# A two-layer graph kernel: visits start at borders of pairs of steps, steps are told of in pairs, and a tile's rows are turned back ahead of the next product

## The reference

```python
def prop(h):
    return segment_sum(h[src] * norm[:, None], dst, num_segments=n)   # norm = -dinv[src] * dinv[dst]
def cheb(x, W0, W1, b):
    return x @ W0 + prop(x) @ W1 + b

h = cheb(x, W1_0, W1_1, b1)                    # 512 -> 512
h = layer_norm(h) * gamma + beta
h = where(h >= 0, h, 0.01 * h)
out = cheb(h, W2_0, W2_1, b2)
result = layer_norm(x + out)                   # no scale, no shift
```

## Time and profile before

| | us |
|---|---|
| median of 3 runs | 2662.75 |
| lowest, highest | 2658.46, 2668.54 |
| the profiled execution | 2677.57 |
| its span | 2675.8 |
| TensorE matmul busy | 2033.7 (76%) |
| GpSimd busy | 1608.5 (60%) |
| VectorE busy | 978.8 (37%) |
| ScalarE busy | 414.5 (15%) |

### The profile page before, as it was taken

The page is one execution under the profiler, slowest core; times in us unless marked ns, Lnnn a source line. Parts: engine busy times, 40 slices in busy tenths (PEclk is TensorE's granted clock), DMA queues, the critical chain, the costliest instruction groups (busy, mean ns, idle before and its releaser), DMA issues.

```text
span 2675.8 us, 28699 instructions
## 1 busy us (share of the span) xinstructions
PE 2033.7 (76%) x8006; PEld 970.8 (36%) x8006; DVE 978.8 (37%) x1503; ACT 414.5 (15%) x844; POOL 1608.5 (60%) x1721
## 2 busy tenths in 40 slices
PE   5258787877888887887884778777787878777887
PEld 5223333333333343443441333333333333333333
DVE  9943333332333333333332233333333333333333
ACT  4401111121222122121221000000000000000001
POOL 0466555666566666666654666666666666666663
PEclk7579888998899899999997889988898888989988
DMA  6576666666576677676756666766666676677674
GB/s 213 193 221 201 195 197 193 198 200 209 178 214 213 205 214 211 200 213 208 208 184 195 195 211 205 215 214 204 213 208 203 212 223 205 206 214 217 207 217 136
DMA packets 191838, 546.41 MB, mean 204 GB/s; under 512 B 32382, under 2 KB 32384, under 8 KB 191692
## 3 DMA queue, kind: packets, MB, share of 16 engines
q0 software_dynamic: 133120, 436.31, 55.3%
q10 hardware_dynamic: 44644, 81.69, 8.5%
q1 hardware_dynamic: 13928, 26.50, 2.7%
HBM read 493.03 MB, written 51.34 MB: 203 GB/s over the span
## 4 chain that ended last, share of the span: by engine, by line
PE 34%; another core or an unknown queue 30%; issue 17%; DVE 11%; ACT 5%; ACTq 1%; POOL 1%; DMA 1%; DVEq 0%; SPq 0%
PE bank L696 14%; PE bank L689 14%; PE bank L751 3%; DVE acc L1136 2%; DVE ring L890 2%; PE bank L638 2%; DVE onehot L1031 1%; DVE work L1012 1%; DVE stats L1067 1%; ACT feat L515 1%; ACT work L494 1%; ACT work L505 1%; DVE ring L892 1%; POOL ring L389 1%
## 5 line engine op out<-in xcount | busy, mean ns | idle before, releaser
L389 POOL DMA_INDIRECT ring<-table,index x1664 | 1574.8, 946 | 941.0 <-issue 468.3
L689 PE MATMUL bank<-ring,onehot 128*128 x4096 | 996.3, 399 | 166.1 <-issue 65.9
L1136 DVE TENSOR_TENSOR acc<-acc,bank 128x512 f32 x512 | 351.4, 686 | 1621.5 <-remote 829.6
L689 PEld LDWEIGHTS bank<-ring,onehot 128*128 128x128 f16 x4096 | 417.8, 102 | 697.8 <-issue 312.0
L696 PE MATMUL bank<-wA,work 128*128 128x512 f32 x784 | 414.8, 679 | 138.4 <-ACT work L494 115.7
L696 PE MATMUL bank<-wB,base_in 128*128 128x512 f32 x784 | 379.0, 628 | 38.2 <-DVE acc L1102 30.8
L1031 DVE TENSOR_TENSOR onehot<-bank,rel 128x1024 f16<-128x1024 f32 x256 | 311.6, 1218 | 0.1
L696 PEld LDWEIGHTS bank<-wA,work 128*128 128x128 f32 x784 | 166.6, 218 | 344.2 <-issue 204.8
L751 PE MATMUL bank<-diag,acc 128*128 128x128 f32 x784 | 135.4, 325 | 168.2 <-DVE acc L1136 98.7
L696 PEld LDWEIGHTS bank<-wB,base_in 128*128 128x128 f32 x784 | 154.5, 204 | 206.2 <-issue 165.5
L751 PEld LDWEIGHTS bank<-diag,acc 128*128 128x128 f32 x784 | 114.4, 224 | 192.8 <-DVE acc L1136 124.5
(11 more groups left out here) (121 smaller groups left out, 672.8 us busy)
## 6 DMA issues: line engine op xcount, KB each, us to landing
ring<-table,index POOLq DMA_INDIRECT x1664
feat<-in_x ACTq DMA_DIRECT2D x96, 256.0 KB
table<-work SPq DMA_DIRECT2D x49, 256.0 KB, 2.7
hidden_t<-feat ACTq DMA_DIRECT2D x49, 256.0 KB
table<-work ACTq DMA_DIRECT2D x49, 256.0 KB
base_in<-hidden_t ACTq DMA_DIRECT2D x49, 256.0 KB
out<-work ACTq DMA_DIRECT2D x48, 256.0 KB
acc<-in_x SPq DMA_DIRECT2D x6, 1792.0 KB, 18.6
```

The costliest lines, as they stand in the source:

```text
L389: nc.gpsimd.indirect_dma_start(out=ring[:, at * ROW:(at + 1) * ROW], out_offset=None, in_=table[l], in_offset=bass.IndirectOffsetOnAxis(ap ...
L689: last = nc.tensor.matmul(bank[n % SUM_BANKS][:, :], hot, ring[:, bass.ds(slot_at + (2 * j + half) * D, D)], start=j + half == 0, stop=j + ...
L1136: nc.vector.tensor_tensor(acc_at, acc_at, bank[n % SUM_BANKS][:, :], ALU.add).then_inc(sums_added, 1)
```

## The change

- `place(v)` is rounded down to an even number of steps, from a first place of 8.75 instead of 8. Of the 48 places 24 stay, 16 are a step later and 8 a step earlier; the distances of 5 (37 times) and 6 (10 times) become 4 (18 times) and 6 (29 times).
- `steps_done` is incremented by 2 at the last matmul of every second step instead of by 1 at every step.
- VectorE's leaky step is due at `place(v)` itself instead of one step later, and the statistics 2 steps later instead of 3.
- In `complete` of layer 0 TensorE does `turn_hidden` first and then the product.
- Four small instructions of VectorE that work out the places at run time follow suit (as many as before).

```diff
-    FIRST_PLACE = -(-STEPS // TILES) + 8 // GROUP
-    PRODUCT_LATER, LEAKY_LATER, STATS_LATER = 2, 1, 3
+    FIRST_PLACE = 35 * 64
+    PRODUCT_LATER, LEAKY_LATER, STATS_LATER = 2, 0, 2
...
-            return min(STEPS, FIRST_PLACE + (v * SPACING >> 8))
+            return min(STEPS, FIRST_PLACE + v * SPACING >> 8 & -BLOCK)
...
-                last.then_inc(steps_done[l], 1)
+                if n % BLOCK == BLOCK - 1:
+                    last.then_inc(steps_done[l], BLOCK)
...
             def complete(l, v):
-                sums_product(l, v)
                 if l == 0 and v > 0:
                     turn_hidden(v)
+                sums_product(l, v)
...
-                link(nc.vector.tensor_scalar(place_i[:, 0:1], part_i[:, :], SPACING, None, ALU.mult))
+                link(nc.vector.tensor_scalar(place_i[:, 0:1], part_i[:, :], SPACING, FIRST_PLACE, ALU.mult, ALU.add))
                 link(nc.vector.tensor_scalar(place_i[:, 1:2], place_i[:, 0:1], 8, None, ALU.arith_shift_right))
-                link(nc.vector.tensor_copy(place_f[:, 0:1], place_i[:, 1:2]))
-                link(nc.vector.tensor_scalar(place_f[:, 1:2], place_f[:, 0:1], float(FIRST_PLACE), None, ALU.add))
+                link(nc.vector.tensor_scalar(place_i[:, 0:1], place_i[:, 1:2], -BLOCK, None, ALU.bitwise_and))
+                link(nc.vector.tensor_copy(place_f[:, 1:2], place_i[:, 0:1]))
```

More of the change, by code:

```diff
@@ L100, in gnn_resnorm_kernel @@
     assert STEPS % LOADED == 0
-    assert EARLY_STEP < FIRST_PLACE and STEPS == 256 and FIRST_PLACE > 0
+    assert EARLY_STEP < FIRST_PLACE >> 8 and STEPS == 256
     assert STEPS % SUM_BANKS == 0 and BOUNDS % SLOTS == 0
@@ L904, in lateness @@
             def lateness():
-                assert all(place(v) == FIRST_PLACE + (v * SPACING >> 8) for v in range(BOUNDS)) and place(BOUNDS) == STEPS
-                link(nc.vector.tensor_scalar(place_i[:, 0:1], part_i[:, :], SPACING, None, ALU.mult))
+                assert all(place(v) == (FIRST_PLACE + v * SPACING >> 8 & -BLOCK) for v in range(BOUNDS)) and place(BOUNDS) == STEPS
+                link(nc.vector.tensor_scalar(place_i[:, 0:1], part_i[:, :], SPACING, FIRST_PLACE, ALU.mult, ALU.add))
                 link(nc.vector.tensor_scalar(place_i[:, 1:2], place_i[:, 0:1], 8, None, ALU.arith_shift_right))
-                link(nc.vector.tensor_copy(place_f[:, 0:1], place_i[:, 1:2]))
-                link(nc.vector.tensor_scalar(place_f[:, 1:2], place_f[:, 0:1], float(FIRST_PLACE), None, ALU.add))
+                link(nc.vector.tensor_scalar(place_i[:, 0:1], place_i[:, 1:2], -BLOCK, None, ALU.bitwise_and))
+                link(nc.vector.tensor_copy(place_f[:, 1:2], place_i[:, 0:1]))
                 link(nc.vector.tensor_tensor(late[0:BOUNDS, 0:1], bound_f[0:BOUNDS, 1:2], place_f[0:BOUNDS, 1:2],
```

## The result

The changed kernel is slower: 2673.36 us against 2659.95 (medians of 20 runs each), ratio 1.005, 95% interval 1.0032 to 1.0068. I had forecast 0.989, in a range from 0.967 to 1.011; 1.005 lies in the range, but on the side to which I gave 0.27. The changed kernel's profiled execution happens to be one of its shorter ones (2664.0 us, span 2662.2) and that of the kernel before a long one (2677.57), so the spans of the two profiles must not be compared; where the waits lie can be.

The account below looks back on a forecast made before the run. No engine was taken as full; TensorE waits in visits for answers to increments seen late. Terms -13 - 10 - 20 - 8 + 16 + 5 = -30 us gave 2647.6 profiled, median 2633; range 2575 to 2692.

Parts of the forecast that it names:

- rival two: TensorE's visit waits form again under other names, so no change: 2663 to 2684 us, put at 2665; chance 0.21.
- Both signs of being wrong: TensorE's idle time before steps grows by 60 us, or waits change names while their sum over both loops stays.
- rival one: Slots freed later in the four-slot ring: half the postponed gathers reach TensorE, +66 us, 2699; chance 0.20.
- Item 1: Layer 0 visits: hidden rows turned while the product waits for ScalarE's copy, -13 us (0 to -29).
- Item 2: Layer 0: the hidden turn's own wait for VectorE's leaky step, now due earlier, -10 us (-20 to +9).
- Item 3: Statistics a step sooner: wait before turning normalised rows -20 us; layer 1's residual add wait -8.
- Item 4: Steps told in pairs: no cost for banks, but the turn of the sums waits for one more add, +16 us.
- Item 5: Slots freed a step later for 104 of 208 groups per layer, little reaching TensorE: +5 us (+3 to +16).
- Item 7: 256 fewer TensorE increments: 0 us; at most 6.7 saved by the skill's 26 ns each, left out of the sum.
- rival three: Lateness itself falls with half the increments of steps, another 80 us gone: 2553 us; chance 0.13.
- items 1 to 6: All terms with bounds, written as -142 and +130 us; the sixth, layer 1's one-hot waits, was 0 (-10 to +10).

Follow-up runs that it names:

- e7: Kernel before with three of four gathers left out of each group but the first four: 1986.11 us.
- e8: Changed kernel with the same three of four gathers left out: 1951.42 us, 0.9825 of e7.
- e16: Changed kernel with three of four gathers left out and steps told one by one: 1948.26 us.
- e18: Kernel before with three of four gathers left out and only the hidden turn put ahead of the product: 2011.74 us.
- e2: Kernel before with only the hidden turn put ahead of the product in layer 0, all gathers: 2297.39 us, 1.0005 of before.
- e4: Kernel before with only the leaky step and statistics each one step earlier, all gathers: 2296.83 us, 1.0001 of before.
- e17: Kernel before with three of four gathers left out and only the early leaky step and statistics: 1949.34 us.
- e13: The changed kernel itself, timed again beside the kernel before: 2305.99 us, 1.0037 of before.
- e14: Changed kernel with steps told one by one again, all gathers: 2305.41 us, 1.0033 of before.
- e12: Kernel before with slots freed only after an even number of steps: 2303.07 us, 1.0028 of before.
- e15: Kernel before with slots freed only after an even number of steps, repeating e12 in another set: 2304.15 us, 1.0029 of before.
- e5: The changed kernel itself, timed again beside the kernel before: 2699.24 us against 2682.24, 1.0065.
- e6: Layer 0 as in the changed kernel, layer 1 as in the kernel before: 2682.44 us, 0.9995 of before.
- e11: Changed kernel with leaky step and statistics back at 1 and 3 steps after the place: 2382.3 us, 1.0365 of before.

## Why the prediction was wrong, by its own steps

**The step that failed is the sum itself**, not its largest terms: that a wait of TensorE's which goes makes the run shorter by as much. It holds only where TensorE's chain is the bound, as in e7, e8, e16 to e18. The sum had -51 us for items 1 to 3 and +21 for the rest; measured were +13.4 us. In late sets the waits formed again (my rival two): idle time in the two stretches 490 and 488 us, with other names. I had that rival's reason, 7.97 us in one piece against savings of 0.6 to 1.8, and gave it 0.21. Both signs of being wrong that I had named came: this one, and 60 us more before the steps, the sign of rival one (it became 108, or 89 if only the odd steps' waits for groups are counted), though not its time of 2699. In prompt sets the gathers are the bound: the waits of visits are fewer (27.8 us for the normalised rows in e2, 2.5 in e4), and taking them away changes nothing.

**Item 1** (hidden turn in the product's wait, -13): in the changed kernel that wait did fall in layer 0, from 79.0 to 25.4 us, but the time did not; alone it is worth nothing in a prompt set (e2, 1.0005) and with few gathers, where the product hardly waits (0.7 us in e7), it can't help.

**Item 2** (its own wait, -10, at worst +9): wrong where it stands alone, +25.6 (e18), through 24 waits and the statistics behind them; right that the early leaky step removes it (e8, e17).

**Item 3** (statistics sooner, -20 and -8): mechanism right in layer 0, size too small: -36.8 with few gathers (e17), nothing in a prompt set (e4). The -8 of layer 1 didn't appear in e17. I had thought that only the long distances would profit; e17 has before's distances and gains all. No late set tried it alone.

**Item 4** (pairs: no bank wait, +16 at the turn of the sums): wrong on both. The turn of the sums didn't get slower, and the steps wait for VectorE's adds 23.7 + 30.2 us by name, where before had 0.7 (78.7 and 7.0 by the place in the step). My 2.6 us of 3.56 took for granted that VectorE is told at the pair's end; told up to 9 to 12 us late, it owes both adds and the one-hots while TensorE is already at the wait of the next pair. With single steps told, the add in question was told one step, 1.78 us, earlier. With prompt increments that wait isn't among e13's.

**Item 5** (slots, +5): late freeing alone, 1.0028 and 1.0029, is 6.4 and 6.6 us in prompt sets, near the +5, but by luck: I had worked it out for late sets, where gathers reach TensorE in part, and in the prompt ones they are the bound. In the changed kernel it can't be told from nothing (e13 against e14, 0.6 us). What it costs in a late set was not timed, as e12 and e15 met prompt ones; the 89 us more before the odd steps say that gathers come through there far more than the 3 to 16 us of my bounds, in waits, if not in time.

**Item 7** and rival three (fewer increments): nothing in them. e16 to e8 goes the other way by 3.2 us (two sets), and where increments are late, halving those of the steps left the changed kernel at 1.005 and 1.0065. The lateness of up to 12 us is not a price per increment: of the 26 ns each of the Trainium skill (TensorE: Matmul & The Clock Gate, "The cost: per-tile semaphore tail") no run here shows anything, for or against.

The bounds of items 1 to 6 add to -119 and +126, not to the -142 and +130 that I wrote; the forecast doesn't hang on it.

What stays open: why layer 1's share costs 0.7% in a late set (e5 against e6). Pairs, places and statistics changed there together, and the kernels that would part them met prompt sets. The new wait of the steps for adds (30.2 us in layer 1) and that for groups behind late slots are candidates, no more. Open too is what made sets late or prompt. Shown is only that it takes both the dense gathers and something outside the kernel: one set had 2682 us with all gathers and no lateness with a quarter of them, another had all gathers and no lateness. Since every set was on another chip, chip and moment can't be told apart. And no version was found that is faster with all gathers: early statistics without pairs (e4) ties with before in a prompt set and was never in a late one.

## What to carry to other kernels

Before adding up an engine's waits, leave out the work of the other engine that might be the bound and time the kernel so: here e7 and e8 would have said that TensorE's chain is 1986 us long, 696 less than the kernel takes in that set, and that 35 us of it were to be had but might not be seen. (Of the 696, about 200 are TensorE's own work at a lower clock: 2033.7 us busy in the first profile of before, 1832.0 in e7's, at mean granted clocks of 0.883 and 0.962.) If several engines go on in the same half microsecond after a long "remote" wait, suspect late messages; savings smaller than the lateness formed again elsewhere here. Telling of work in pairs is only safe if everything that hangs on it, adds, statistics and slots, is due at the pair's border: with the leaky step and the statistics off it (e11) the kernel took 3.65% more than before, the changed kernel 0.37% (e13, another set).

## What the runs showed of the hardware that I had not expected

The same kernel took 2660 to 2682 us in some sets and 2296 to 2299 in others, 14% less, each kind repeating within about 1%. What differs in the profiles is when TensorE's increments are seen: up to 12 us after the recorded end of the matmul (step at 1008.89, add at 1021.07) while GpSimd issued gathers 1.25 us apart, and at once with a quarter of the gathers (the add starts 0.13 us after its step's end by the median of those that waited, in e7). TensorE's granted clock was 0.88 on the mean of the changed kernel's first profile, with its pauses, and 0.94 in e2's; for the same matmuls it was busy 2033.8 and 1910.2 us.
